# An edge layer's histogram and lane-count products, dealt in three parts over a block of TensorE's order

## The chip, the cores and the metric

The kernel runs on one core of a Trainium2 chip. The metric is the device time of one execution in microseconds (us), the median of several executions. Lower is better.

## The reference

A graph network of four layers on 12,500 nodes with 64 features and 400,000 edges (`src`, `dst`, sorted by `dst`). The first, the edge layer, is the one that matters here:

```
x_i = x[dst]; x_j = x[src]
edge_features = jnp.concatenate([x_i, x_j - x_i], axis=-1)
h = jax.nn.relu(edge_features @ W1 + b1)
edge_messages = h @ W2 + b2
out = jax.ops.segment_max(edge_messages, dst, num_segments=x.shape[0])
```

The three layers behind it are a graph convolution (normed by the out-degree of `src` and the in-degree of `dst`), a two-hop mean aggregation and a weighted aggregation, each with a layer norm, a ReLU and a residual sum around it. The convolution needs the out-degree of every node, which is a histogram of `src`, and the dense layers need, for every chunk of edges, how often each (row, node) pair occurs.

## The kernel before, in words

The edges lie in 128 lanes of 3,125, and the edge layer walks through them in 125 blocks of K = 25 columns (128 x 25 edges). Five blocks (slots r = 0 to 4) make one pass of a hardware loop (`body0`), and each engine has a loop of its own; semaphores alone tie them together.

Per block the engines do this:

- **GpSimd (POOL)** gathers the rows of the 25 columns by indirect DMA (L632) and one row of keys per lane (L640, tile `crow`). It runs ahead of the others by up to the ring's five slots.
- **VectorE (DVE)** adds the fill to the gathered rows (L1424), copies the block's keys (`lane_keys`, L1435), and then builds one-hot batches with `row_onehots` (L685). Each batch is two instructions, one over 128 classes (`ohq`, 2,048 or 1,152 elements a partition) and one over 98 classes (`ohr`, 1,568 or 882). The first two batches, `hist_batch` 0 (16 columns) and 1 (9 columns), are for the histogram. Eight more, `count_batch` v = 0 to 7 (16 columns each), are for the block counts. Between the batches stand the steps of two scans (L1393), the fill of the next block and the running maximum of this one; the latter takes the products in `om`.
- **TensorE (PE)** multiplies the one-hots. `hist_counts` adds, per column, two products into `hist` and two into `cnt`, both parts of the PSUM bank `mixed`. `block_counts` v makes 32 products in four groups of eight into the two banks `bk`. `turn` q transposes eight columns of the gathered rows into `tp` (four transposes, L1929), and a product q with `w_diag` (L1952) writes `om`; q runs over 0 to 3 (eight, eight, eight columns, and one).
- **ScalarE (ACT)** copies the turned keys into `eqw` (L1745), applies the ReLU from `tp` to `hT` (L1753), moves each group of `bk` to the staging buffer (L1737), and issues the stores.

The one-hots have two buffers, shared by both kinds of batch: `hist_batch` h writes buffer h, and `count_batch` v writes buffer v mod 2. So `count_batch` 0 waits until all products of `hist_batch` 0 are done, and `count_batch` 1 until all of `hist_batch` 1 are (semaphore `histed`); every later one waits for `block_counts` v - 2 (semaphore `banked`). On DVE:

```
if v < 2:
    wait(e, "histed", b * 2 + (v + 1))
else:
    wait(e, "banked", b * CW + (v - 1) * 4)
```

TensorE's order in a block is written out by hand in `body0` of `block.tensor` (L1932 to L1958): two transposes of the keys, `turn` 0, `hist_counts` 0 (64 products), `hist_counts` 1 (36 products), `turn` 1, product 0, `block_counts` 0, `turn` 2, product 1, `block_counts` 1 and 2, and so on to `block_counts` 7.

Of the kernel before, what the change touches and what calls it, by code (L numbers as in the profile page):

```python
# [19 lines left out]
K = 25  # L20
# [7 lines left out]
VS = 16  # L28
# [9 lines left out]
HIST = [range(0, VS), range(VS, K)]  # L38
# [19 lines left out]
def build(nc, x, src, dst, edge_weight, l0_w1, l0_b1, l0_w2, l0_b2, l1_w, l1_b,  # L58
# [7 lines left out]
    with ctx:  # L66
# [8 lines left out]
        def sem(name):  # L75

            if name not in sems:
                sems[name] = ctx.enter_context(nc.semaphore(name))
            return sems[name]
# [216 lines left out]
        def wait(e, name, n):  # L296

            if not (isinstance(n, int) and n <= 0):
                e.wait_ge(sem(name), n)  # L299

        def gate(e):

            e.sem_inc(sem("gate_" + e.engine.name), 1)
# [643 lines left out]
        def pairs(cols):  # L947
            return [cols[a:a + 2] for a in range(0, len(cols), 2)]
# [918 lines left out]
        def _(e):  # L1867
            e.wait_ge(sem("const"), 1)
            e.wait_ge(sem("checked"), 1)
            for c in range(2):  # L1870
                last = e.matmul(pb[0:1, 0:1], bad[:, c:c + 1], ones[:, 0:1], start=c == 0, stop=c == 1)
# [9 lines left out]
            for g in range(NGROUPS // 2):  # L1881
                e.wait_ge(sem("rows_vector"), g + 1)
                for k in range(2 * NT):
                    last = e.matmul(pa[:, :], mark_u[:, k // 2, :, k % 2], mark_v[:, k // 2, :, k % 2], start=g + k == 0,
                                    stop=g == NGROUPS // 2 - 1 and k == 2 * NT - 1, skip_group_check=True)
# [9 lines left out]
            def halves(to, by_q, by_r, start, stop):  # L1895

                for k in range(0, P, D):
                    last = e.matmul(to[k:k + D, :], by_q[:, k:k + D], by_r, start=start, stop=stop, skip_group_check=True)  # L1898
                return last

            def hist_counts(b, h):

                wait(e, "batched", b * (VB + 2) + (h + 1))
                gate(e)
                for c in range(len(HIST[h])):
                    first = isinstance(b, int) and b + h + c == 0
                    halves(hist, ohq[h][:, c, :], ohr[h][:, c, :], first, c == len(HIST[h]) - 1)
                    last = halves(cnt, ident_b, ohr[h][:, c, :], False, c == len(HIST[h]) - 1)
                last.then_inc(sem("histed"), 1)

            def block_counts(b, v):

                wait(e, "batched", b * (VB + 2) + (v + 3))
                gate(e)
                for s in range(4):
                    wait(e, "bank_out", b * CW + (v * 4 + s - 1))
                    gate(e)
                    for m in range(4):
                        last = halves(bk[s % 2][:, m * TILES:(m + 1) * TILES], ohq[v % 2][:, s * 4 + m, :],
                                      ohr[v % 2][:, s * 4 + m, :], True, True)  # L1920
                    last.then_inc(sem("banked"), 1)

            def turn(b, r, q):

                wait(e, "copied0", b * NQ + (q - 1))
                gate(e)
                for k, c in enumerate(pairs(MAXQ[q])):
                    m = len(c) * D
                    last = e.transpose(tp[q % 2][0:m, k * P:(k + 1) * P],  # L1929
                                       ring[:, r, c[0]:c[-1] + 1, :], ident[:, :])  # L1930
                last.then_inc(sem("turned0"), 1)

            def body0(i):
                for r in range(R):
                    b = i * R + r
                    wait(e, "keyed", b + 1)
                    wait(e, "keys_copied", b)
                    gate(e)
                    e.transpose(kp[:, 0:P], ckey[:, :], ident[:, :])
                    e.transpose(kp[:, P:2 * P], crow[:, r, CH:2 * CH], ident[:, :]).then_inc(sem("keys_turned"), 1)  # L1940
                    wait(e, "summed0", b + 1)
                    turn(b, r, 0)
                    hist_counts(b, 0)
                    hist_counts(b, 1)
                    for q, cols in enumerate(MAXQ):
                        if q + 1 < NQ:
                            turn(b, r, q + 1)
                        wait(e, "copied0", b * NQ + (q + 1))
                        wait(e, "taken0", b * NQ + (q - 1))
                        for k, c in enumerate(pairs(cols)):  # L1950
                            m = len(c) * D
                            last = e.matmul(om[q % 2][:, k * P:k * P + m], hT[0:m, q % 2, k * P:(k + 1) * P],  # L1952
                                            w_diag[0:m, 0:m], start=True, stop=True)
                        last.then_inc(sem("products0"), 1)
                        for v in range(max(2 * q - 1, 0), min(2 * q + 1, VB)):
                            block_counts(b, v)
                    for v in range(2 * NQ - 1, VB):
                        block_counts(b, v)  # L1958
            loop(e, body0)
            fix_tensor(e, 0)  # L1960
            e.wait_ge(sem("taken0"), BLOCKS * NQ)
# [6 lines left out]
            for a in range(2):  # L1968
                last = e.transpose(pa[:, a * D:(a + 1) * D], w_lastT[:, a, :], ident[0:D, 0:D])
# [62 lines left out]
```

## Time and profile before

| | us |
|---|---|
| median of 3 runs | 18454.92 |
| lowest, highest | 18447.9, 18476.08 |
| span of the profiled execution | 13809.8 |

No time of the profiled execution as a whole is given beside its span. The median of the runs lies 4645 us above the span, and the profile shows nothing of what fills that. The edge layer's loop takes about 4.7 ms of the span. Over the whole span PE is busy 51%, DVE 66%, ACT 43% and POOL 57%. A busy share is an average over stages, so it has to be read in the edge layer's loop alone, where the rows below come from.

### The profile page before, as it was taken

The numbers are of one execution on the slowest core, as the hardware profiler recorded it, in microseconds if no ns is written. First come the engines' busy times: TensorE is split into PE (matmuls) and PEld (weight loads), VectorE is DVE, ScalarE is ACT, GpSimd is POOL, SyncE is SP. The second block draws the span as 40 slices with busy tenths as digits, with TensorE's granted clock in tenths as the row PEclk, the third lists the DMA queues.
The fourth block names the chain that finished last, engine by engine and source line by source line (L and its number), as shares of the span: only waits on it lengthen the run. The fifth ranks groups of instructions, "written<-read, shape, count | busy, mean of one in ns | idle before, by whom it ended". The sixth has DMA issues, their size and how long they took to land. (4 is left out here: it accounts for less than half of the span.)

```text
span 13809.8 us, 283975 instructions
## 1 busy us (share of the span) xinstructions
PE 7082.0 (51%) x96792; PEld 5084.7 (37%) x96792; DVE 9045.7 (66%) x17848; ACT 5948.2 (43%) x10705; POOL 7815.4 (57%) x7194
## 2 busy tenths in 40 slices
PE   2266666666666663998899999700000000000066
PEld 1155555555555552554455555400000000000055
DVE  5388888888888886444444344466666666666585
ACT  0144444444444443776777677522222222222201
POOL 5677777777777773111111111367777777777700
PEclk9866666666666666999899899755555555555598
DMA  7333333333333333886688588422222222222197
GB/s 308 144 112 113 112 114 114 119 112 112 113 112 115 115 114 94 261 265 220 200 263 267 172 265 263 160 72 66 63 66 66 66 63 66 63 63 66 60 361 241
DMA packets 1274431, 1981.83 MB, mean 144 GB/s; under 512 B 256937, under 2 KB 987918, under 8 KB 1268737
## 3 DMA queue, kind: packets, MB, share of 16 engines
q1 hardware_dynamic: 867553, 1059.78, 24.4%
q10 hardware_dynamic: 174288, 612.09, 12.0%
q0 software_dynamic: 231664, 297.80, 8.1%
q8 instruction: 558, 9.14, 0.3%
q14 instruction: 368, 3.01, 0.1%
HBM read 1167.21 MB, written 815.55 MB: 144 GB/s over the span
## 5 line engine op out<-in xcount | busy, mean ns | idle before, releaser
L632 POOL DMA_INDIRECT RF<-tab_edge_b,idx x3125 | 3541.2, 1133 | 1030.6 <-issue 948.6
L1180 POOL DMA_INDIRECT records<-RF,idx x3125 | 3130.6, 1002 | 984.5 <-issue 984.5
L1737 ACT ACTIVATE X<-bk 128x392 uint8<-128x392 f32 x4000 | 1782.6, 495 | 1565.0 <-PE bk L1898 1548.0
L685 DVE TENSOR_TENSOR HM<-iota_b,eqw 128x2048 bf16<-128x2048 bf16 x2000 | 2201.7, 1101 | 342.7 <-PE bk L1898 197.6
L1898 PE MATMUL bk<-HM 128*64 128x98 bf16 x32000 | 1583.2, 247 | 1306.7 <-ACT X L1737 672.8
L1898 PE MATMUL kp<-HM,ident_b 128*64 128x98 bf16 x6250 | 281.7, 283 | 3805.4 <-DVEq L1646 3805.4
L876 POOL DMA_INDIRECT agg<-RF,lastT x372 | 536.9, 1443 | 2856.9 <-ACT RF L808 2766.0
L769 PE MATMUL tp<-HM,RF 128*64 128x512 bf16 x12276 | 2001.2, 379 | 7.9 <-ACT HM L728 2.0
L1898 PEld LDWEIGHTS bk<-HM 128*64 128x64 bf16 x32000 | 1239.8, 134 | 1653.2 <-issue 1571.3
L1898 PEld LDWEIGHTS kp<-HM,ident_b 128*64 128x64 bf16 x6250 | 261.7, 168 | 3826.3 <-issue 3826.3
L775 PE MATMUL om<-HM,RF 128*64 128x512 bf16 x6138 | 1442.3, 379 | 0.0
L769 PE MATMUL tp<-RF 128*64 128x512 bf16 x5952 | 1032.7, 381 | 201.4 <-ACT RF L728 201.4
L769 PEld LDWEIGHTS tp<-HM,RF 128*64 128x64 bf16 x12276 | 854.2, 110 | 651.6 <-issue 52.3
L730 DVE CAST HM<-dst_f 128x4096 bf16<-128x4096 uint8 x186 | 426.8, 2294 | 739.1 <-DMA dst_f<-counts 390.1
L1828 ACT ACTIVATE RF<-qblk 128x50 f32<-128x50 f32 x125 | 31.7, 254 | 1978.9 <-DMA records<-RF,idx 1904.2
L1393 DVE SCALAR_TENSOR_TENSOR RF<-RF,dupjunk 128x64 f32<-128x64 f32 x3124 | 865.8, 277 | 27.3
L1393 DVE SCALAR_TENSOR_TENSOR RF<-RF,dupjunk,om 128x64 f32<-128x64 f32 x3124 | 841.2, 269 | 0.4
L728 ACT ACTIVATE RF<-dst_f 128x4096 bf16<-128x4096 uint8 x186 | 672.7, 3617 | 343.1 <-PE tp L769 342.0
L728 ACT ACTIVATE HM<-dst_f 128x4096 bf16<-128x4096 uint8 (+1 forms) x186 | 702.2, 3822 | 102.5 <-PE tp L769 102.5
L775 PE MATMUL om<-RF 128*64 128x512 bf16 x2976 | 722.6, 381 | 0.0
L728 ACT ACTIVATE HM<-crow 128x4096 bf16<-128x4096 uint8 x186 | 670.6, 3606 | 6.4 <-DMA crow<-counts 4.5
L1898 PE MATMUL mixed<-HM 128*64 128x98 bf16 x6250 | 498.6, 272 | 329.8 <-DVE HM L685 278.2
(362 smaller groups left out, 14805.4 us busy)
## 6 DMA issues: line engine op xcount, KB each, us to landing
dst_f<-counts SPq DMA_DIRECT2D x465, 512.0 KB, 4.6
RF<-first_rows SPq DMA_DIRECT2D x250, 800.0 KB
counts<-X ACTq DMA_DIRECT2D x250, 784.0 KB
records<-RF ACTq DMA_DIRECT2D x88, 1960.0 KB, 8.2
RF<-records SPq DMA_DIRECT2D x220, 784.0 KB
crow<-counts SPq DMA_DIRECT2D x279, 512.0 KB, 4.7
first_rows<-RF ACTq DMA_DIRECT2D x25, 4000.0 KB, 49.5
edge_rows<-RF ACTq DMA_DIRECT2D x125, 800.0 KB, 8.0
```

The lines of the kernel that those rows point to most:

```text
L632: e.indirect_dma_start(out=ring[:, r, j, :], out_offset=None, in_=table[:, :], in_offset=bass.IndirectOffsetOnAxis(ap=idx[:, r, j:j + 1], ...
L685: return e.tensor_tensor(to[:, 0:n, :].rearrange("p k (q h) -> p k q h", h=2), iota_b[:, 0:m].rearrange("p (q h) -> p q h", h=2).unsqueeze ...
L728: e.activation(to, of, ACT.Copy).then_inc(sem("widened_A"), 1)
L730: e.tensor_copy(to, of).then_inc(sem("widened_D"), 1)
L769: last = e.matmul(tp[u][k * D:(k + 1) * D, :], hi_mid[:, t, k * D:(k + 1) * D], part, start=t == 0, stop=t == TILES - 1, skip_group_check= ...
L775: return e.matmul(om[u][k * D:(k + 1) * D, :], low[:, t, :], part, start=t < 2, stop=t >= TILES - 2, skip_group_check=True)
L876: e.indirect_dma_start(out=agg[:, :], out_offset=bass.IndirectOffsetOnAxis(ap=lastT[:, g * GB + k:g * GB + k + 1], axis=0), in_=out_rows[g ...
L1180: e.indirect_dma_start(out=records[:, :], out_offset=bass.IndirectOffsetOnAxis(ap=idx2[:, r, j:j + 1], axis=0), in_=msgs[MSG_OF[r]][:, j, ...
L1393: e.scalar_tensor_tensor(out=buf[:, r, j, :], in0=prev, scalar=mask[:, j:j + 1], in1=this, op0=op0, op1=op1).then_inc(sem(chain.name), 1)
L1737: e.activation(staged[u].rearrange("p (r k) -> p r k", k=P)[:, :, k:k + 4], bk[s % 2][:, 0:4 * TILES].rearrange("p (k r) -> p r k", k=4), ...
L1828: e.activation(msgs[MSG_OF[r]][:, :, RW - 2:RW], qblk[:, r, :].unsqueeze(2).broadcast_to([P, K, 2]), ACT.Copy)
L1898: last = e.matmul(to[k:k + D, :], by_q[:, k:k + D], by_r, start=start, stop=stop, skip_group_check=True)
```

## The change

TensorE's list of a block is put in another order. `hist_counts` gets the columns to do as an argument. The first 8 columns of `hist_batch` 0 stand where both batches stood; the other 8 come behind `turn` 1; the 9 columns of `hist_batch` 1 come behind `block_counts` 0. The number of instructions stays the same on every engine, as do the two increments of `histed` per block: the first comes behind the sixteenth column of batch 0, the second behind the ninth of batch 1.

```
-            def hist_counts(b, h):
+            def hist_counts(b, h, cols):
...
-                for c in range(len(HIST[h])):
+                for c in cols:
...
-                last.then_inc(sem("histed"), 1)
+                if cols[-1] == len(HIST[h]) - 1:
+                    last.then_inc(sem("histed"), 1)
...
                     turn(b, r, 0)
-                    hist_counts(b, 0)
-                    hist_counts(b, 1)
+                    hist_counts(b, 0, range(8))
                     for q, cols in enumerate(MAXQ):
                         if q + 1 < NQ:
                             turn(b, r, q + 1)
+                        if q == 0:
+                            hist_counts(b, 0, range(8, VS))
                         wait(e, "copied0", b * NQ + (q + 1))
...
                         for v in range(max(2 * q - 1, 0), min(2 * q + 1, VB)):
                             block_counts(b, v)
+                        if q == 0:
+                            hist_counts(b, 1, range(K - VS))
```

The first place is TensorE's order in the second block, around the end of the histogram's products (`mixed`), before the change. The last products of batch 1 are followed by `turn` 1 (`tp1`), product 0 (`om0`) and `block_counts` 0 (`bk0`, `bk1`):

```order
L1898 MATMUL mixed<-HM 64x98 x2
L1898 MATMUL mixed<-HM,ident_b 64x98 x2
L1929 MATMUL tp1<-ident,RF 128x128 [waits copied0]
L1929 MATMUL tp1<-ident,RF 128x128 x3
L1952 MATMUL om0<-w_diag,hT 128x128 [waits taken0,copied0]
L1952 MATMUL om0<-w_diag,hT 128x128 x3
L1898 MATMUL bk0<-HM 64x98 [waits batched,bank_out]
L1898 MATMUL bk0<-HM 64x98 x7
```

With the change, `turn` 1 stands in the middle of batch 0, at the same place of TensorE's order (the row with `batched` opens the second half of batch 0):

```order
L1898 MATMUL mixed<-HM 64x98 x2
L1898 MATMUL mixed<-HM,ident_b 64x98 x2
L1930 MATMUL tp1<-ident,RF 128x128 [waits copied0]
L1930 MATMUL tp1<-ident,RF 128x128 x3
L1898 MATMUL mixed<-HM 64x98 [waits batched]
L1898 MATMUL mixed<-HM 64x98
```

The four transposes of `turn` 1 have moved ahead of the second half of batch 0, whose end gives the first increment of `histed`. The second place, also on TensorE with the change, is where batch 1 begins:

```order
L1954 MATMUL om0<-w_diag,hT 128x128 [waits taken0,copied0]
L1954 MATMUL om0<-w_diag,hT 128x128 x3
L1898 MATMUL bk0<-HM 64x98 [waits batched,bank_out]
L1898 MATMUL bk0<-HM 64x98 x7
L1898 MATMUL bk1<-HM 64x98 [waits bank_out]
L1898 MATMUL bk1<-HM 64x98 x7
L1898 MATMUL bk0<-HM 64x98 [waits bank_out]
L1898 MATMUL bk0<-HM 64x98 x7
L1898 MATMUL bk1<-HM 64x98 [waits bank_out]
L1898 MATMUL bk1<-HM 64x98 x7
L1898 MATMUL mixed<-HM 64x98 [waits batched]
L1898 MATMUL mixed<-HM 64x98
```

All 36 products of batch 1 have moved behind product 0 and behind the four groups of `block_counts` 0. The orders of DVE, ACT, POOL and SP are the same as before. The third place is DVE, unchanged, at the two one-hot batches that wait for `histed` (`count_batch` 0 and 1, with the scans' steps between them):

```order
L685 TENSOR_TENSOR HM<-iota_b,eqw 128x2048 [waits keys_copied,histed]
L1393 SCALAR_TENSOR_TENSOR RF<-RF,dupjunk 128x64 [waits v_fill] x2
L685 TENSOR_TENSOR HM<-iota_b,eqw 128x1568
L1393 SCALAR_TENSOR_TENSOR RF<-RF,dupjunk 128x64 [waits v_fill] x2
L685 TENSOR_TENSOR HM<-iota_b,eqw 128x2048 [waits products0,histed]
```

## Rows read from the trace of the kernel before

**Rows 1.** Edge loop: one line's instructions on DVE, one per block (L1422)
```profile
L1422 DVE TENSOR_SCALAR ckey<-crow,node128T x125: 273/303/309, 563.1 to 5235.2; 128x128 f32<-128x128 f32 x125
```
**Rows 2.** Busy time by stretch; PE, PEld, DVE, ACT, POOL, granted clock, DMA share, GB/s
```profile
3000.00:4000.00 1000.00, 620.67 (x10454) 523.26 (x10451) 871.01 (x2004) 441.60 (x979) 775.99 (x691) 0.68 0.36 112
```
**Rows 3.** Waits of DVE and POOL, 1500 to 4500 us: total, times, longest
```profile
DVE HM L685 <- PE bk L1898: 129.5, 238, 0.9
DVE lane_keys L1435 <- issue: 75.2, 16, 5.5
DVE HM L685 <- PE mixed L1898: 56.6, 71, 3.9
...
DVE HM L685 <- PE om L1952: 15.9, 30, 0.9
```
**Rows 4.** POOL's groups of instructions, 1500 to 4500 us: busy, mean ns, idle
```profile
L632 POOL DMA_INDIRECT RF<-tab_edge_b,idx x1988 | 2254.1, 1134 | 632.1 <-issue 603.4 <-DMA cix<-chunk_lin 28.7
L640 POOL DMA_INDIRECT crow<-kr,cix x80 | 90.9, 1137 | 24.4 <-issue 24.4
```
**Rows 5.** Timeline of DVE in one block: start, length, what, idle before
```profile
3062.96 1.22 DVE L685 TENSOR_TENSOR HM<-iota_b,eqw 128x2048 bf16<-128x2048 bf16 x1 [0.37 <-PE mixed L1898]
...
3064.62 0.97 DVE L685 TENSOR_TENSOR HM<-iota_b,eqw 128x1568 bf16<-128x1568 bf16 x1
...
3066.22 1.22 DVE L685 TENSOR_TENSOR HM<-iota_b,eqw 128x2048 bf16<-128x2048 bf16 x1
...
3073.18 1.27 DVE L685 TENSOR_TENSOR HM<-iota_b,eqw 128x2048 bf16<-128x2048 bf16 x1 [0.52 <-PE bk L1898]
```
**Rows 6.** Timeline of PE in the same block
```profile
3056.71 1.06 PE L1929 MATMUL tp<-ident,RF 128*128 128x128 f32 x4
3059.99 0.29 PE L1898 MATMUL mixed<-HM 128*64 128x98 bf16 x2 [2.22 <-DVE HM L685]
...
3062.50 0.32 PE L1898 MATMUL mixed<-HM,ident_b 128*64 128x98 bf16 x2
3062.58 0.31 PE L1898 MATMUL mixed<-HM 128*64 128x98 bf16 x2
...
3063.96 0.27 PE L1898 MATMUL mixed<-HM,ident_b 128*64 128x98 bf16 x2
3064.16 0.66 PE L1929 MATMUL tp<-ident,RF 128*128 128x128 f32 x4
3064.66 1.06 PE L1952 MATMUL om<-w_diag,hT 128*128 128x128 f32 x8
3065.97 0.55 PE L1898 MATMUL bk<-HM 128*64 128x98 bf16 x16 [0.26 <-issue]
3067.12 0.76 PE L1898 MATMUL bk<-HM 128*64 128x98 bf16 x16 [0.59 <-ACT X L1737]
3067.81 0.66 PE L1929 MATMUL tp<-ident,RF 128*128 128x128 f32 x4
...
3070.44 0.76 PE L1898 MATMUL bk<-HM 128*64 128x98 bf16 x16 [0.53 <-ACT X L1737]
```
**Rows 7.** Busy time by stretch, the histogram's products, then what follows, two blocks
```profile
3059.90:3062.60 2.70, 2.61 (x65) 2.64 (x67) 2.58 (x8) 1.09 (x2) 2.09 (x3) 0.50 1.01 408
...
3065.90:3067.90 2.00, 1.31 (x33) 1.05 (x34) 1.89 (x5) 1.16 (x3) 1.70 (x2) 1.00 0.10 22
...
3026.60:3027.20 0.60, 0.60 (x29) 0.53 (x23) 0.60 (x1) 0.00 (x0) 0.60 (x1) 1.00 0.29 55
```
**Rows 8.** Timeline of PE, histogram's products at the high clock (slot 0)
```profile
3026.59 0.23 PE L1898 MATMUL mixed<-HM 128*64 128x98 bf16 x2
...
3026.99 0.23 PE L1898 MATMUL mixed<-HM,ident_b 128*64 128x98 bf16 x2
```
**Rows 9.** Timeline of PE, one block-counts batch at the low clock
```profile
3083.33 0.86 PE L1898 MATMUL bk<-HM 128*64 128x98 bf16 x16 [0.87 <-DVE HM L685]
3084.64 0.93 PE L1898 MATMUL bk<-HM 128*64 128x98 bf16 x16 [0.45 <-ACT X L1737]
```

## The prediction

> **What bounds the kernel now.** I read the busy time by stretches first, then the waits of the edge layer's loop, then one block as a timeline. The change touches nothing outside that loop. VectorE (DVE) passes L1422 once per block, so 124 periods lie between 563.1 and 5235.2 us [rows 1]: 37.68 us per block. In a stretch in the middle DVE is busy 87% and TensorE (PE) 62% [rows 2], so per block DVE works 32.8 us and stands 4.9 us, and PE has about 14 us to spare. That does not make PE's order free. The reader should see who waits for whom [rows 3]. In 3000 us, or 79.5 blocks (1988 + 80 gathers at 26 a block [rows 4]), DVE waited 56.6 us for products into `mixed`, 0.7 us per block, 15.9 us for products into `om`, 0.2 us, and 75.2 us at the loop's turn, where it waits for nothing that the profile shows.
>
> The largest entry, 129.5 us on `bk` in 238 waits, is three waits a block of 0.52 to 0.54 us. I read them as a fixed cost of the hand-over between two groups of columns, not as PE's lateness: the batch at 3073.18 us stood 0.52 us [rows 5], while the block counts that it needs (`block_counts` 1) had ended at 3070.44 + 0.76 = 3071.20 us [rows 6], two microseconds before. So nothing that the change does to PE gives these back.
>
> GpSimd (POOL) is nearly as full as DVE. Its gathers and the gaps between them fill the window (2254.1 + 90.9 + 632.1 + 24.4 = 3001.5 us), and only 28.7 us of that, 0.36 us per block, are spent waiting for an index [rows 4]. A gather and the gap behind it cost 1.134 + 0.304 us, or 26 x 1.438 = 37.4 us per block. A faster DVE could therefore gain at most about 0.3 us per block. A slower DVE loses all that it loses, because POOL only waits for it.
>
> So DVE's own chain sets the pace: its work, its fixed gaps, and the places where PE ends last. The question is what the new order does at those places.
>
> **The change, part by part.** No instruction is added or taken away on any engine, and only PE's order changes. PE's semaphore waits move with the instructions; the second half of batch 0 waits for a batch that has long been made, and that costs nothing while its cover (the first half has already run on the same batch) is there.
>
> Step 1: `turn` 1 goes ahead of the second half of batch 0. DVE's `count_batch` 0 writes the buffer of batch 0 and waits for its last product. PE already ended last there: batch 0 started at 3059.99, its 32nd row at 3062.50 ended at 3062.82, and DVE started at 3062.96 after standing 0.37 us [rows 5, 6]. So the release takes 0.14 us and the transposes lie in the open. At the high clock they take 0.50 us (3064.16 to the start of the next group at 3064.66) [rows 6]. At the low clock a group of four is 1.06 us instead of 0.66 us [rows 6], so 0.90 us. Batch 0's products ran at 0.50 granted, the lower level (1.2 GHz) [rows 7], so I take 0.8 us, nearer the low clock, and keep 0.5 and 0.9 as ends.
>
> Step 2: batch 1 goes behind `block_counts` 0. This is the costly one. `count_batch` 1 writes the buffer of batch 1, and DVE must wait there for batch 1's last product. Before, those 36 products ran in PE's slack, from 3062.58 to 3063.96 + 0.27 = 3064.23 [rows 6], two microseconds before DVE wanted the buffer at 3066.22 [rows 5]. Now they stand behind `block_counts` 0, and that waits for `count_batch` 0 to be made. It ended at 3064.62 + 0.97 = 3065.59; PE started on it at 3065.97 and came to its next group at 3067.81 [rows 5, 6]. At that moment batch 1 could start. At the high clock its 18 rows of products, spaced (3026.99 - 3026.59) / 9 = 0.044 us [rows 8], take 17 x 0.044 + 0.23 = 0.98 us, so DVE starts at 67.81 + 0.98 + 0.14 = 68.93 instead of 66.22: a stall of 2.7 us. At the low clock they take 1.65 us (3062.58 to 3064.23), and the stall is 3.4 us. If `block_counts` 0 itself also runs at the low clock, it takes 2.24 us (3083.33 to 3085.57) [rows 9] instead of 1.91 us (3065.97 to 3067.88) [rows 6], and the stall is 3.7 us. DVE issues in order, so the two one-hots, the scans' steps and all later batches stand behind this wait, and PE and ACT, which feed on DVE's batches, wait with it. I take 2.7 us: `block_counts` 0 ran at 1.00 granted in this block [rows 7], after a dense run of PE from 3059.99 us on, and that dense run keeps most of its length (the first 64 products, the transposes and product 0).
>
> Step 3: product 0 comes earlier, by the 36 products that have left its front. DVE waits for it only 0.2 us per block [rows 3], and that wait goes, since DVE now stands at the same place for `histed` anyway: -0.2 us. `turn` 2 and product 1 now come behind batch 1, by about a microsecond. DVE wants product 1 three microseconds later, after it has built two batches (3.3 us from one to the next by the starts at 3062.96 and 3066.22 [rows 5]), so that lies beside DVE's work. If it did not, the wait would be at `count_batch` 3, with up to a microsecond.
>
> What POOL, ACT and the stores do is hidden in DVE's time before, and more so with a longer block.
>
> Sum: 0.8 + 2.7 - 0.2 = 3.3 us per block, 125 blocks, 412 us. Against the profiled execution that is a span of 13,810 + 412 = 14,222 us. Of its whole time only the span is given, and the median of the runs is 4645 us longer. I leave that rest as it is, since no part of the program changes outside the loop, and predict 18,455 + 412 = 18,867 us. The ends: 0.5 + 2.7 - 0.2 = 3.0 us gives 18,830; 0.9 + 3.7 - 0.2 = 4.4 us gives 19,005. A little more could be lost below: if a quarter of the 1.6 us on `bk` were PE's after all and vanished behind the stall, 2.6 us would be left, 18,780.
>
> **The rivals.**
>
> Rival A, the clock is lost. The same mechanism, but the row of products is cut and PE stands about two microseconds behind product 0, waiting for a batch. Then `block_counts` 0 and batch 1 run at the lower level: 4.4 us per block, 19,005 us. For it: at 3083 us, after waits of 0.8 us and more, the counts run at the low clock [rows 9]. Against it: 3065.9 to 3067.9 us had the full clock right behind such a dense run [rows 7]. The Trainium skill, "TensorE: Matmul & The Clock Gate" (Part 1: The HAM clock gate), says that the default state is throttled and that only activity releases it, which speaks for this rival and against cutting rows of products; by it the sum would be the 4.4 us.
>
> Rival B, not slower: POOL sets the pace in the runs, and the stall is hidden. The place is POOL's 26 gathers per block. The stall vanishes when they take more than 37.68 + 3.3 = 41.0 us, that is when each costs (41.0 - 37.4) / 26 = 0.14 us more than in this profile. For it: 4645 us of the median are in no row. If a tenth of them lay in this loop's gathers, that would be 465 / 125 = 3.7 us per block, and the point would be passed. Then the time stays at 18,455 us. Against it: in the profile DVE never waits for a gather [rows 3], and nothing shows that the rest lies in this loop.
>
> Rival C, faster. The earlier product 0 counts and batch 1 is not missed, for example because PE gets to it before DVE needs the buffer. The gain is the 0.2 us on `om` and a part of the 0.7 us on `mixed`, capped by POOL at 0.36 us per block: 45 us, 18,410 us. Against it: the order puts batch 1 behind work that DVE must first make, and DVE asks for the buffer 0.6 us after making it.
>
> That the change does nothing can be excluded from the order of the instructions: only PE's differs, at the places shown.
>
> **How the numbers follow.** Two tenths of a percent, 37 us, is about what a measurement of this kernel can tell from no change. My forecast has 0.70, rival A 0.20, rival B 0.07 and rival C 0.03. The first two are slower by over 0.2%: 0.90; B is the same: 0.07; C is faster: 0.03. The range goes from 18,780 (the lower bound of the sum) to 19,020 (rival A and a little), which leaves out B, C and a part of the tails, together less than 2 in 10.
>
> **What the changed profile would show.** Periods of L1422 of 41.0 us. In DVE's waits, `mixed` goes from 0.7 us per block to about 4.2 us (twice per block instead of once), `om` goes to nothing, and the three waits of 0.52 us stay. PE waits about two microseconds for DVE behind product 0, then runs `block_counts` 0 and batch 1 in one go. POOL's wait for an index grows by 3.3 us per block. Steps 1 and 2 are wrong if the batch at `count_batch` 0 stands less than 0.8 us or `count_batch` 1 less than 2 us; the forecast is wrong if `mixed` grows and the period does not, or if DVE starts to wait for gathers.

## The result, and the profile after it

The changed kernel takes 18,809 us in the median of its runs (18,806 to 18,822), the kernel before beside it 18,465 us. The ratio is 1.0185, with a 95% interval of 1.0171 to 1.0199: 344 us slower, where 412 us were forecast. The sign and the size are right. The profile after the change shows another picture than the one on which the forecast stood. Its span is 18,804 us, so here the span is the time, and nothing lies outside it.

One line's instructions on DVE, one per block, after the change (columns as in [rows 1]):

```profile
L1422 DVE TENSOR_SCALAR ckey<-crow,node128T x125: 275/279/287, 615.8 to 9075.8; 128x128 f32<-128x128 f32 x125
```

The block period is (9075.8 - 615.8) / 124 = 68.2 us, where the first profile had 37.68 us [rows 1] and the forecast 41.0 us. A difference of 30.5 us can't be the work of a change that costs 344 / 125 = 2.75 us per block.

The waits of DVE after the change, 2000 to 8000 us, that is 6000 / 68.23 = 87.9 blocks (columns as in [rows 3]; "remote" is a releaser that the profile can't name):

```profile
DVE HM L685 <- remote: 2099.9, 77, 31.4
DVE HM L685 <- PE mixed L1898: 680.5, 96, 26.7
DVE HM L685 <- PE bk L1898: 141.6, 260, 0.9
```

The waits on `bk` stayed at 1.6 us per block, as predicted. Those on `om` are gone, as predicted. The new thing is a long wait in nearly every block, 19 to 32 us and 26.8 us in the mean. One block shows where it stands, in DVE's timeline:

```profile
4056.74 0.61 DVE L685 TENSOR_TENSOR HM<-iota_b,lane_keys 128x882 bf16<-128x882 bf16 x1
...
4084.77 1.23 DVE L685 TENSOR_TENSOR HM<-iota_b,eqw 128x2048 bf16<-128x2048 bf16 x1 [26.90 <-remote]
...
4086.43 0.97 DVE L685 TENSOR_TENSOR HM<-iota_b,eqw 128x1568 bf16<-128x1568 bf16 x1
...
4091.65 1.23 DVE L685 TENSOR_TENSOR HM<-iota_b,eqw 128x2048 bf16<-128x2048 bf16 x1 [3.74 <-PE mixed L1898]
```

`count_batch` 0 stands 26.9 us, for the end of batch 0; `count_batch` 1 stands 3.74 us, for the end of batch 1. The second is the stall of step 2. The first has nothing like it in [rows 5]. PE's timeline in the same stretch shows what it does meanwhile:

```profile
4060.00 0.29 PE L1898 MATMUL mixed<-HM,ident_b 128*64 128x98 bf16 x2
4060.08 0.28 PE L1898 MATMUL mixed<-HM 128*64 128x98 bf16 x1
...
4062.05 0.24 PE L1898 MATMUL mixed<-HM 128*64 128x98 bf16 x1 [1.04 <-issue]
...
4063.51 1.08 PE L1954 MATMUL om<-w_diag,hT 128*128 128x128 f32 x2 [0.40 <-issue]
...
4067.04 0.58 PE L1954 MATMUL om<-w_diag,hT 128*128 128x128 f32 x1 [0.34 <-issue]
4087.79 0.86 PE L1898 MATMUL bk<-HM 128*64 128x98 bf16 x16 [20.16 <-DVE HM L685]
4089.10 0.93 PE L1898 MATMUL bk<-HM 128*64 128x98 bf16 x16 [0.45 <-ACT X L1737]
4089.79 0.32 PE L1898 MATMUL mixed<-HM 128*64 128x98 bf16 x2
...
4091.18 0.32 PE L1898 MATMUL mixed<-HM,ident_b 128*64 128x98 bf16 x2
```

From 4060 us on, PE's instructions come out singly, about one or two in 1.3 us, though PE waits for nothing that the profile can name ("issue"). The last record of batch 0 ends at about 4062.4 us and the last of product 0 at 4067.62 us. Yet the trace's updates of the two semaphores that tell DVE of these ends stand at 4084.64 and 4084.73 us, 22 and 17 us later. In between the profile has PE waiting 20.16 us for DVE's next batch, while DVE waits for PE. In the first profile the semaphore of batch 0 moves 0.01 us after the recorded end of its last product; in this one the delay is 20.6 us in the median block. I call the whole of this the crawl: the products come out singly, and the word of their end comes late. Whether PE issues slowly, or ends slowly, or is only recorded so, the rows do not tell. POOL gathers all the while:

```profile
4047.83 0.94 POOL L632 DMA_INDIRECT RF<-tab_edge_b,idx  x1 [37.99 <-DMA cix<-chunk_lin]
...
4079.99 0.95 POOL L640 DMA_INDIRECT crow<-kr,cix  x1 [0.30 <-issue]
4118.08 0.94 POOL L632 DMA_INDIRECT RF<-tab_edge_b,idx  x1 [37.14 <-DMA cix<-chunk_lin]
```

The block's 26 gathers run from 4047.83 to 4080.94 us, the two semaphores move about four microseconds later, and then POOL stands 37 us until DVE has finished the block and the next index is loaded.

### The profile page after: what moved, and what is told of

The parts are those of the page before. It is cut to its first block and busy times, and to the rows that moved or that the text cites. A ratio compares the mean times of both kernels' runs of the same rounds, so it can differ in the third digit from the quotient of the medians.

```text
span 18803.8 us, 284100 instructions
## 1 busy us (share of the span) xinstructions
PE 7823.1 (42%) x96792; PEld 5606.2 (30%) x96792; DVE 9014.3 (48%) x17848; ACT 5966.2 (32%) x10705; POOL 7232.8 (38%) x7194
## 5 line engine op out<-in xcount | busy, mean ns | idle before, releaser
L632 POOL DMA_INDIRECT RF<-tab_edge_b,idx x3125 | 3044.2, 974 | 5334.2 <-DMA cix<-chunk_lin 4335.9
L1898 PE MATMUL bk<-HM 128*64 128x98 bf16 x32000 | 1664.1, 260 | 3435.3 <-DVE HM L685 2543.4
L1898 PEld LDWEIGHTS bk<-HM 128*64 128x64 bf16 x32000 | 1324.5, 143 | 3809.5 <-issue 3757.6
L1898 PE MATMUL kp<-HM,ident_b 128*64 128x98 bf16 x6250 | 377.2, 280 | 4789.1 <-DVEq L1646 3763.6
L775 PE MATMUL om<-HM,RF 128*64 128x512 bf16 x6138 | 1325.8, 379 | 0.0
L1954 PE MATMUL om<-w_diag,hT 128*128 128x128 f32 (+1 forms) x3250 | 811.4, 391 | 443.4 <-issue 438.0
L1898 PE MATMUL mixed<-HM 128*64 128x98 bf16 x6250 | 641.0, 278 | 554.7 <-issue 287.5
L1954 PEld LDWEIGHTS om<-w_diag,hT 128*128 128x128 f32 (+1 forms) x3250 | 696.9, 293 | 522.6 <-issue 491.5
L1898 PE MATMUL mixed<-HM,ident_b 128*64 128x98 bf16 x6250 | 650.0, 278 | 370.0 <-issue 367.6
L685 DVE TENSOR_TENSOR HM<-iota_b,rtwice 128x2450 bf16<-128x2450 bf16 x125 | 179.3, 1434 | 1159.5 <-remote 1147.9
```

What stands on the lines that cost most here:

```text
L632: e.indirect_dma_start(out=ring[:, r, j, :], out_offset=None, in_=table[:, :], in_offset=bass.IndirectOffsetOnAxis(ap=idx[:, r, j:j + 1], ...
L685: return e.tensor_tensor(to[:, 0:n, :].rearrange("p k (q h) -> p k q h", h=2), iota_b[:, 0:m].rearrange("p (q h) -> p q h", h=2).unsqueeze ...
L775: return e.matmul(om[u][k * D:(k + 1) * D, :], low[:, t, :], part, start=t < 2, stop=t >= TILES - 2, skip_group_check=True)
```

## The experiments

The twelve runs were timed in three groups of four; the table at the end of this section has each run's group, and of the three runs without gathers the first two are in the second group and the last in the third. The kernel before, timed beside each group, had a median of 18,617, 18,472 and 18,616 us. So times are compared inside a group, and kernels of different groups by their ratios to the kernel before.

**Is the crawl the change's?** The kernel before, with no edit.

> The kernel before, unchanged, profiled again, because its first profile has a span of 13,810 us beside a median of 18,465 us, while the changed kernel's span, 18,804 us, is 2 us under its time. Theory A (the first profile came from an execution without a stall that the timed ones have): span about 18,460 us, block period about 65 us, and a wait of some 24 us per block at count_batch 0 like the 26.6 us in the changed kernel. Theory B (the span is 13,810 us again): period 37.7 us and no such wait, and then the stall belongs to the change.

Measured: 18,631 us, ratio 0.9999 (0.9987 to 1.0010), span 18,632 us. Its blocks and the waits of its DVE, 2000 to 8000 us:

```profile
L1422 DVE TENSOR_SCALAR ckey<-crow,node128T x125: 279/282/287, 619.7 to 8852.3; 128x128 f32<-128x128 f32 x125
```
```profile
DVE HM L685 <- remote: 2080.5, 78, 31.5
DVE HM L685 <- PE om L1952: 352.4, 89, 14.1
DVE HM L685 <- PE mixed L1898: 187.1, 7, 27.0
DVE HM L685 <- PE bk L1898: 146.4, 269, 0.9
DVE HM L685 <- issue: 104.3, 24, 26.9
```

Theory A holds. The period is (8852.3 - 619.7) / 124 = 66.4 us, and the crawl is in the kernel before as well. The first profile, with its span of 13,810 us, showed an execution unlike the timed ones. Of the 4823 us between the two spans, 8232.6 - 4672.1 = 3560 us lie in the edge loop [rows 1]; the other 1.3 ms lie outside it and are not explained here.

With this the waits of the change can be compared in two like traces. DVE stands (2080.5 + 352.4 + 187.1 + 104.3) / 90.4 = 30.1 us per block at its waits on PE's histogram and product 0 before, and (2099.9 + 680.5 + 28.2 + 0.5) / 87.9 = 32.0 us after (the last two from entries on `issue` and on DVE itself). The difference of 1.9 us is that of the two periods, 68.2 and 66.4 us. It is less than 2.75 us; the two traces come from different groups, and the kernel before was 166 us slower in this one (18,631 against 18,465 us), so this comparison is good for the places and not for the size. One thing the forecast could not see: before, DVE stood 352.4 / 90.4 = 3.9 us per block for product 0, not 0.2 us [rows 3]. Product 0 stood behind batch 1 there, and both behind the crawl. The change takes that wait away and puts one for batch 1 in its place, 3.7 us in the median block and 5.2 us in the mean.

Busy time by stretch shows the crawl next to its absence (columns as in [rows 2]). In the kernel before, again, during the gathers and with most of them past:

```profile
4434.20:4454.00 19.80, 5.15 (x42) 2.71 (x42) 0.22 (x1) 0.00 (x0) 14.98 (x16) 0.50 0.25 68
4456.00:4476.00 20.00, 9.34 (x120) 7.41 (x121) 8.75 (x20) 5.65 (x12) 4.23 (x5) 0.67 0.06 14
```

That is 42 products in 19.8 us, in which POOL issued 16 gathers: PE's recorded pace is two or three products per gather. At the same granted clock the first profile had 65 in 2.7 us, with POOL just as busy [rows 7]. So neither the clock nor a want of work explains the crawl.

**The two steps, one at a time.** Step 1 alone:

```
hist_counts(b, 0, range(8))
...
turn(b, r, 1)
hist_counts(b, 0, range(8, VS))
hist_counts(b, 1, range(K - VS))
... product 0, block_counts 0
```

> Step 1 alone: turn 1 in the middle of batch 0, batch 1 right behind it, ahead of product 0. Theory A (the prediction's sum): DVE waits 0.8 us per block longer at count_batch 0, 100 us, ratio 1.005. Theory B (a long stall at that place in the timed runs takes the transposes in): no change within 0.2%, ratio 1.000.

Measured: ratio 1.0000 (0.9990 to 1.0010). Theory B has the number: alone, step 1 costs nothing in the timed runs. Its reason does not hold, though. DVE stood 29.9 us at `count_batch` 0 instead of 26.2 us, and 0.2 us at `count_batch` 1 instead of 4.1 us (the table below): 3.7 us were lost at the first place and 3.9 us won at the second, where the wait for product 0 had been.

Step 2 alone:

```
hist_counts(b, 0, range(VS))
... turn 1, product 0, block_counts 0
hist_counts(b, 1, range(K - VS))
```

> Step 2 alone: batch 0 in one row, batch 1 behind block_counts 0. Theory A (the prediction's sum): 2.5 us per block, 312 us, ratio 1.017, and the wait at count_batch 1 about 3 us. Theory B (step 1 costs nothing and step 2 all of the 344 us measured): ratio 1.0185. If batch 1 behind block_counts 0 were not the cause: within 0.2%.

Measured: ratio 1.0118 (1.0101 to 1.0136), and 1.0112 (1.0095 to 1.0129) when it was run once more. Step 2 alone is slower, by 219 to 244 us or about 1.9 us per block; both theories had expected more. The wait at `count_batch` 1 was 3.7 us in the median block and 4.8 us in the mean, but only 0.7 us of that mean is new, since 4.1 us had been waited there for product 0. Another 0.9 us stand ahead of `count_batch` 0, where step 2 changes nothing in PE's order; no run explains them.

**Where must batch 1 stand?** Ahead of `block_counts` 0, behind product 0:

```
hist_counts(b, 0, range(VS))
... turn 1, product 0
hist_counts(b, 1, range(K - VS))
... block_counts 0
```

> Batch 0 in one row, then turn 1 and product 0, then batch 1, ahead of block_counts 0: batch 1 still moves behind product 0, but runs while PE waits for count_batch 0 to be made. Theory A (only the place behind block_counts 0 costs): no stall at count_batch 1, ratio 0.998 to 1.000. Theory B (any batch 1 behind product 0 comes too late): ratio over 1.005, with a wait over 1 us at count_batch 1.

Measured: ratio 0.9926 (0.9910 to 0.9943), 126 us faster than the kernel before. Theory A is right in its mechanism and too small in its gain. Repeated in the third group:

> Batch 0 in one row, turn 1, product 0, batch 1, then block_counts 0, once more. Theory A (the gain of 0.7% is real: product 0 and batch 1 are both in place when the crawl ends): ratio 0.991 to 0.995. Theory B (it was that chip's scatter): within 0.2% of 1.

Measured: 18,483 us, ratio 0.9922 (0.9903 to 0.9942). The gain is real. Its waits, 2000 to 8000 us:

```profile
DVE HM L685 <- remote: 2251.6, 79, 31.5
DVE HM L685 <- PE mixed L1898: 366.7, 55, 27.0
```

With the entries on `issue` (56.1 us) and on DVE (7.8 us) these are 29.2 us per block (6000 / 65.3 = 91.9 blocks), 0.9 us less than in the kernel before of the first group. At `count_batch` 1 DVE stands 1.2 us in the mean and 0.1 us in the median block, instead of 4.1 us, and 1.8 us more at `count_batch` 0. This version is faster than both kernels.

Batch 1 between the second and the third of the four groups of `block_counts` 0:

```
for s in range(4):
    if s == 2 and v == 0: hist_counts(b, 1, range(K - VS))
```

> A smaller dose of step 2: batch 0 in one row, batch 1 between the second and the third group of block_counts 0. Theory A (the stall at count_batch 1 is the time that PE spends between the making of count_batch 0 and batch 1's last product): about 1 us less than with batch 1 behind all four groups, so ratio 1.004 to 1.007. Theory B (any place behind product 0 at which PE waits for count_batch 0 costs the same): ratio 1.012.

Measured: ratio 1.0015 (1.0006 to 1.0025). Two groups fewer in front of batch 1 save most of the price. That is theory A's direction, and more than its amount. With batch 1 ahead of all four groups, in their middle and behind them, the ratios are 0.993, 1.0015 and 1.012, so the price grows with what stands in front of batch 1. The waits do not bear out theory A's reason here: DVE stood 7.3 us at `count_batch` 1, longer than with all four groups in front, and 22.5 us at `count_batch` 0, shorter than in any other trace that shows the crawl. Why the crawl divides itself so is open.

**Is it the gathers?** The 25 gathers of a block became one plain DMA of the same size into the same tile, in the kernel before and in the changed one. The gathered rows are then others than the reference's.

```
-            for j in range(K):
-                e.indirect_dma_start(out=ring[:, r, j, :], ...)
+            e.dma_start(ring[:, r, :, :], table.rearrange("(p t) f -> p t f", p=P)[:, 0:K, :])
```

> The kernel before with the 25 indirect gathers of a block replaced by one plain DMA of 25 rows a lane into the same tile (so the gathered rows are others than the reference's, the rest of the work is the same); the key gather stays. Theory A (PE crawls because POOL's gathers run beside it, which costs some 29 us per block): block period 37 to 39 us as in the first profile, no wait over 2 us at count_batch 0, time about 15,000 us. Theory B (the crawl comes from something else, such as the stores or PE's instruction loading): period still over 60 us.

Measured: 14,988 us, ratio 0.8113 (0.8099 to 0.8126).

```profile
L1420 DVE TENSOR_SCALAR ckey<-crow,node128T x125: 275/279/286, 614.9 to 5269.2; 128x128 f32<-128x128 f32 x125
```
```profile
DVE HM L683 <- PE bk L1896: 129.0, 237, 0.9
...
DVE HM L683 <- PE mixed L1896: 58.1, 64, 4.1
...
DVE HM L683 <- PE om L1950: 20.7, 41, 0.8
```

The first line is the block line (two lines higher in this source), the others are DVE's waits from 1500 to 4500 us. The period is 37.5 us, and the waits are those of [rows 3] nearly to the number: 0.7 us per block on `mixed`, 0.26 us on `om`. Theory A: with the gathers the crawl goes, though the stores and PE's instructions are unchanged. The loop is as in the first profile, but the span is 14,975 us and not 13,810 us, so the first profile was shorter outside the loop as well. The run also makes a place where the prediction's own sum can be tried.

> The changed kernel with the same replacement (the gathered rows are others than the reference's). Against the run before it: theory A (without the crawl both steps lie in the open, as the prediction had it): period longer by 3.0 to 3.7 us, 375 to 460 us in all, a wait at count_batch 0 0.8 us longer and one of about 3 us at count_batch 1. Theory B (step 1 is free here too): longer by 2.0 to 2.7 us, 250 to 340 us.

Measured: 15,557 us, 568 us more than the run before it, or 4.5 us per block.

```profile
L1420 DVE TENSOR_SCALAR ckey<-crow,node128T x125: 276/279/286, 616.8 to 5816.7; 128x128 f32<-128x128 f32 x125
```
```profile
DVE HM L683 <- PE mixed L1896: 389.6, 144, 5.4
DVE HM L683 <- PE bk L1896: 115.8, 213, 0.9
```

The period is 41.9 us, 4.4 us longer. The waits on `mixed` are 389.6 / 71.5 = 5.4 us per block instead of 0.7 us, in two places instead of one; those on `om` are gone, and those on `bk` are unchanged at 1.6 us. Both steps lie in the open, as theory A has it, but it was 0.7 us too low at its upper end. By place, DVE stands 2.0 us at `count_batch` 0 instead of 0.8 us, and 3.5 us at `count_batch` 1 instead of 0.3 us. One block of this run shows the second stall, and the granted clock from PE's wait for `count_batch` 0 into batch 1 (columns as in [rows 2]):

```profile
3026.74 1.23 DVE L683 TENSOR_TENSOR HM<-iota_b,eqw 128x2048 bf16<-128x2048 bf16 x1 [3.57 <-PE mixed L1896]
```
```profile
3021.00:3023.00 2.00, 0.02 (x1) 0.00 (x0) 1.93 (x6) 0.00 (x0) 0.00 (x0) 1.00 0.98 402
3023.05:3023.70 0.65, 0.64 (x16) 0.45 (x16) 0.12 (x1) 0.15 (x1) 0.00 (x0) 0.74 0.29 118
3024.20:3025.00 0.80, 0.80 (x19) 0.79 (x21) 0.00 (x0) 0.37 (x2) 0.00 (x0) 0.50 0.02 8
```

`block_counts` 0 begins at the full clock, the clock falls inside it, and batch 1 runs at the lower level. The granted clock was full when `block_counts` 0 began in 112 of 119 blocks, and at its lower level when batch 1 ended in 107.

> Step 1 alone with the gathers replaced as in the two runs without gathers (the gathered rows are others than the reference's). Against a median of 14,988 us for the kernel before so treated: theory A (step 1 lies in the open when there is no crawl): 1.0 to 1.3 us per block, 125 to 160 us more, and the wait at count_batch 0 rises from 0.7 to about 1.9 us. Theory B (step 1 costs nothing in itself): within 40 us.

Measured: 15,130 us, 142 us above the 14,988 us of the kernel before so treated. These two times are from different groups, between which the kernel before moved by 144 us, and by their ratios (0.8125 and 0.8113) the two are only some 20 us apart. So the times decide nothing here, and the reading rests on the loop in the trace.

```profile
L1420 DVE TENSOR_SCALAR ckey<-crow,node128T x125: 281/282/286, 615.2 to 5382.9; 128x128 f32<-128x128 f32 x125
```
```profile
DVE HM L683 <- PE mixed L1896: 144.0, 78, 4.3
```

The period is 38.45 us, 0.9 us longer, and the wait on `mixed` is 144.0 / 78 = 1.85 us instead of 0.73 us. Theory A, by the trace: without the crawl step 1 costs about 1 us per block. Step 2 then has the remaining 41.9 - 38.45 = 3.5 us.

**Do the steps add in the timed runs?**

> The changed kernel itself, for a comparison with step 2 alone on one chip. Theory A (step 1 is hidden by the crawl): ratio 1.011 to 1.013, as step 2 alone. Theory B (the steps add): 1.016 or more.

Measured: ratio 1.0177 (1.0157 to 1.0197), in theory B's range. Step 2 alone had 1.0118, but in another group, so both were timed once more in one group.

> Step 2 alone once more, now on the same chip as the whole change. Theory A (step 1 is hidden behind the crawl): ratio as the whole change within 0.2%. Theory B (the steps add, by about 0.8 us per block): the whole change 0.5% above this run.

> The whole change, on the same chip as step 2 alone. Theory A: within 0.2% of it. Theory B: 0.5% above it. Against the kernel before: 1.017 to 1.019 as twice before.

Measured: 1.0112 (1.0095 to 1.0129) for step 2 alone and 1.0224 (1.0207 to 1.0242) for the whole change. Theory A falls here: in this group step 1 costs another 187 us on top of step 2, 1.5 us per block, though alone it cost nothing in the first. The whole change itself missed the 1.017 to 1.019 that was expected of it; its interval lies above those of both earlier measurements. The waits of DVE, 2000 to 8000 us, step 2 alone:

```profile
DVE HM L685 <- remote: 2040.2, 75, 31.4
DVE HM L685 <- PE mixed L1898: 553.7, 91, 26.7
DVE HM L685 <- issue: 217.3, 21, 27.0
```

and the whole change in the same group:

```profile
DVE HM L685 <- remote: 2311.1, 76, 31.6
DVE HM L685 <- PE mixed L1898: 564.2, 94, 30.4
...
DVE HM L685 <- issue: 8.4, 20, 0.4
```

The table has, for the blocks 5 to 123 of each trace, the mean idle time of DVE just ahead of `count_batch` 0 and of `count_batch` 1, and the block period, all in us. The last column counts the blocks, of 118, in which the semaphore for batch 0's end moved before the block's last gather was issued.

| kernel | group | `count_batch` 0 | `count_batch` 1 | period | early |
|---|---|---|---|---|---|
| before, first profile | | 0.8 | 0.3 | 37.7 | |
| before, again | 1 | 26.2 | 4.1 | 66.4 | 43 |
| step 1 alone | 1 | 29.9 | 0.2 | 66.3 | 0 |
| step 2 alone | 1 | 27.1 | 4.8 | 68.2 | 35 |
| batch 1 ahead of the counts | 1 | 28.1 | 1.0 | 65.3 | 16 |
| batch 1 in their middle | 2 | 22.5 | 7.3 | 65.9 | 59 |
| batch 1 ahead of the counts, again | 3 | 28.0 | 1.2 | 65.3 | 21 |
| step 2 alone, again | 3 | 26.6 | 5.2 | 68.1 | 32 |
| whole change, first result | | 26.8 | 5.2 | 68.2 | 39 |
| whole change, again | 2 | 26.9 | 5.1 | 68.1 | 33 |
| whole change, third time | 3 | 29.9 | 3.7 | 69.8 | 0 |

Ahead of `count_batch` 0 step 1 has nearly the same effect in the third group as alone: 3.3 us more, against 3.7 us. What differs is what comes back at `count_batch` 1. Alone it was 3.9 us, the whole wait for product 0. On top of step 2 that wait has gone already, and only 1.5 us come back. In the other two traces of the whole change step 1 shows no effect at all. There the end of batch 0 reached DVE before the last gather in 39 and 33 of 118 blocks; in the trace of the third group, and with step 1 alone, it did so in none. Which of the two happens sets what step 1 costs. Why it shifts from run to run stays open.

## Why the prediction was right, and where it was not

**The mechanism: right where the prediction looked, but the picture was not that of the timed runs.** PE ended last at `count_batch` 1 instead of in its slack. The wait stands at the predicted instruction, with batch 1's products as its releaser. Putting batch 1 ahead of `block_counts` 0, with step 1 undone as well, turns the loss into a gain. The crawl, which makes up most of DVE's idle time in the timed runs, is in no term of the prediction, and that the sum came near is in part luck (see step 3).

**Step 1, 0.8 us: a little low without the crawl, another thing with it.** Without gathers the period grew by 0.9 us, and the stall at `count_batch` 0 by 1.1 to 1.2 us, a little over the prediction's upper end of 0.9 us. In the timed runs it was 0 alone and 1.5 us on top of step 2. The premise that PE ends last at `count_batch` 0 was true; what it ends last behind was the crawl.

**Step 2, 2.7 us: the term was mis-sized, by the clock.** The failed choice is "I take 2.7 us: `block_counts` 0 ran at 1.00 granted": from the clock of `block_counts` 0 it took that of batch 1 behind it. Without gathers DVE stood 3.5 us at `count_batch` 1. `block_counts` 0 did begin at the full clock there, but it fell inside it, after PE had stood two microseconds, and batch 1 ran at the lower level. That is the middle one of the prediction's three workings, 3.4 us. So of rival A's mechanism one half was seen in these runs, batch 1 at 1.2 GHz, and the other half, `block_counts` 0 at the lower level, was not. That the whole sum came to 4.4 us, rival A's very number, has another make-up than rival A's: 1.2 us at `count_batch` 0 and 3.2 us more than before at `count_batch` 1. In the timed runs the clock was mostly low there. In the block of the changed kernel shown above `block_counts` 0 took 4089.10 + 0.93 - 4087.79 = 2.24 us, batch 1's rows are 0.08 us apart instead of 0.044 us [rows 8], and the stall was 3.74 us, the prediction's upper end. There the cut row is not what took the clock: `block_counts` 0 began at the lower level in 93 of 119 blocks of the kernel before, too, behind the crawl. The Trainium skill, "TensorE: Matmul & The Clock Gate" (Part 1: The HAM clock gate), has the throttled clock as the default and activity as what releases it. The traces agree: the granted clock was 0.50 in the stretch of the crawl from 4434.20 us, in which PE was busy 5.15 of 19.80 us.

**Step 3, -0.2 us: far too small in the timed runs.** There the wait for product 0 was 3.9 us per block, and it went. This, and not a small stall, is why the price was below 4.4 us per block. In the final sum two errors met: a stall too small by 1 us in the median block of the changed kernel (by 2.5 us in its mean), and a gain too small by 3.7 us. That they nearly cancelled is luck.

**Rival B: the place was right, the effect wrong.** The hidden 4645 us did lie mostly in this loop and had to do with POOL's gathers. But they did not make POOL the engine that sets the pace with slack behind it; they made PE crawl while they ran, and DVE's stall stayed in the open behind them. In most blocks of the timed runs the order of events is this: the 26 gathers end 36 us after L1422, the end of batch 0 reaches DVE 3 to 5 us later (in 67 of 118 blocks of the changed kernel, in all of them in the third group), then comes what PE still has to do for `count_batch` 1, and from there to the next L1422 it is 23.4 us in every kernel. A change to PE's list is priced only in the stretch ahead of `count_batch` 1.

**Rival C** did not occur with this order, but it did with batch 1 ahead of `block_counts` 0. There its limit of 45 us, POOL's slack, did not hold either: 126 and 134 us were gained, since POOL stands 3066.8 / 90 = 34 us per block in the second profile of the kernel before (its waits for an index, 2000 to 8000 us).

**The fixed hand-over of 0.52 us** on `bk` was read rightly: 1.6 us per block in every kernel.

## What to carry to other kernels

When two engines trade buffers, a block of work moved out of an engine's slack must come back before its buffer is asked for: put it where the engine waits anyway (here behind product 0 and ahead of the counts), not behind the work that the other engine has still to hand over. When a profile's span lies a quarter below the timed runs, take a second profile before any sum is made from it; a right total can come from two wrong terms. Price a stall at both clock levels, each piece for itself: here the piece right behind PE's two idle microseconds began at the full clock, and the next one had the lower.

## What the hardware showed that was not expected

While POOL issued its indirect gathers, PE is recorded with 42 products in 19.8 us instead of 65 in 2.7 us, at the same granted clock, with its inputs made and nothing to wait for that the profile names. The semaphores behind them moved up to 29 us after the last recorded product. With the gathers replaced by one plain DMA both were gone, and the kernel took 14,988 us instead of 18,472 us. DVE and ACT instructions kept their durations (a one-hot in a block with the crawl took 1.23 us, one in the first profile 1.22 us [rows 5]; ACT's ReLU had a median of 0.597 us in both profiles of the kernel before). That the gathers bring it about is shown; by what (their descriptors, their packets, or the recording of either) is not, and the first profile, in which the same gathers ran beside PE without a crawl [rows 7], stays unexplained. It is not tried here whether other indirect DMAs, such as the scatter in the last layer, do the same to PE.
